# Second attention on one Trainium2 core: value products of two k-tiles side by side, row sums from the exponentials on GpSimd and VectorE

## The chip, the cores and the metric

The kernel runs on 1 core of one Trainium2 chip. The metric is the device time of one launch in microseconds (us). Both kernels get the same inputs and must return the same output.

## The reference, cut to what matters

The program is two transformer layers on a 2048 x 512 matrix. Each layer has a layer norm, an attention and a second branch. The change is in the second layer's attention (`_L1_ffn_ref`), which has 16 heads of 32 columns:

```python
scores = jnp.einsum('bhtd,bhsd->bhts', Qf, Kf) * scale
causal = jnp.tril(jnp.ones((Tx, Tx), dtype=bool))
scores = jnp.where(causal[None, None], scores, jnp.finfo(scores.dtype).min)
attn = jax.nn.softmax(scores, axis=-1)
out = jnp.einsum('bhts,bhsd->bhtd', attn, V)
y = out.transpose(0, 2, 1, 3).reshape(Bx, Tx, C)
return y @ Wp
```

T is 2048 and the batch is 1. All of it is float32.

## The kernel before, in words

The stages follow each other, each in a block of its own: `project0` and `ternary_mlp`, the first attention (`attention` with ATTN0, tiles named a_, about 566 to 1530 us), `project_out`, `gated_cumsum` and `project1` (to about 2004 us), the second attention (`attention` with ATTN1, about 2020 to 2717 us, also named a_), and `project_out` once more (w_). Both attentions use one function.

The second attention has 8 groups of 2 heads. Each group runs two passes over the scores.

Pass 1 finds the row maxima. A block is (g, i, kc): the 128 queries of tile i against up to 512 keys of chunk kc, both heads. TensorE writes the scores of both heads into one of two 128 x 1024 PSUM tiles ps_1 (`max_scores`, L620, with the causal mask added by L628 on the diagonal), and VectorE reduces them to 128 x 2 maxima (`maxima`, L706). There are 320 blocks. After each chunk c of 4 query tiles, `flip` (L637) turns the maxima into rows, `take_rows` (L723, L725) splits them, and SyncE carries them through DRAM into two extra rows of q (`put_rows`, L515, L520). So pass 2 gets scores with the maximum already taken off.

Pass 2 has 320 steps (g, c, t): 512 queries of chunk c against the 128 keys of tile t, t from 0 to 4c+3, so 4, 8, 12 and 16 steps for the four chunks and 40 for a group. In the last four steps of a chunk (the diagonal) only 512, 384, 256 and 128 columns remain (`first_col`). In a step TensorE writes transposed scores for each head into one of three PSUM tiles (`scores`, L649, mask L654), ScalarE takes the exponential into one of 6 SBUF tiles ex (L601), and TensorE multiplies with v (`times_v`, L668), one step behind. v_st has 64 columns for a head (VW=64): 32 of v and 32 ones. So each product writes 64 rows of ps_o: 32 of output and 32 copies of the row sum. The two heads of a step use rows 0 to 63 and 64 to 127. At a chunk's end ScalarE copies ps_o to SBUF (`stage`, L589); SyncE stores output and one sum row a head (L529, L530), loads the sums again as 128 x 8 (L539), VectorE inverts them (L733), SyncE stores them (L545); `project_out` reads them.

The order on each engine is written out. TensorE runs in step s: scores of head 0, the pass 1 block n = s + LEAD, scores of head 1, value products of step s-1. LEAD is 21: 21 blocks run ahead of step 0 and none are left for the last 21 steps. VectorE runs the maxima in the same order. `max_scores` waits until the block two places before has been reduced (`taken1`). All DMAs of the stage are on SyncE's queue. GpSimd does nothing in it after three memsets (L578).

In the first attention (HG=4, VW=32) a step has four heads, and each product writes 32 rows of ps_o: four column groups of TensorE in one `times_v`.

Of the kernel before, what the change touches and what calls it, by code (L numbers as in the profile page):

```python
# [14 lines left out]
F32 = mybir.dt.float32  # L15
# [22 lines left out]
ATTN0 = dict(HG=4, KH=1, VH=1, DH=16, VW=32, SCALE=16 ** -0.5, GROUPS=8, HALVES=2)  # L38
ATTN1 = dict(HG=2, KH=2, VH=2, DH=32, VW=64, SCALE=32 ** -0.5, GROUPS=8, HALVES=1)
QK0 = 768  # L40
# [78 lines left out]
def project0(nc, keep, A, X, xh, xl, ones_mean, eps, D):  # L119


    with ExitStack() as ctx:
# [46 lines left out]
        summed = sem("summed")  # L169
        sums_done = sem("sums_done")  # L170

# [155 lines left out]
        def _(dve):  # L327
# [56 lines left out]
            dve.wait_ge(summed, n_pieces)  # L384
            dve.tensor_reduce(A["abs_sums"][:, :], parts[:, :, :], AX.X, ALU.add).then_inc(sums_done, 1)

# [17 lines left out]
def attention(nc, shared, name, cfg, D, n_layer, neg_ident, mask):  # L404
# [42 lines left out]
    with ExitStack() as ctx:  # L447
# [247 lines left out]
        def _(dve):  # L695
# [39 lines left out]
            for s in range(-1, len(STEP_LIST) + Z_DELAY + 1):  # L735
                for n in SLOTS.get(s, ()):
                    if n in FLIP_AT:
                        take_rows(n)
                    if n < len(BLOCKS):
                        maxima(n)  # L740
                        g, i, kc, p = BLOCKS[n]
                        if LAST_BLOCK[g, i // TPC] == n:
                            whole_max(g, i // TPC, n)
                if s - Z_DELAY in LAST_STEP:
                    invert(*LAST_STEP[s - Z_DELAY])
# [443 lines left out]
def project1(nc, keep, reused, xh, xl, D):  # L1189


    with ExitStack() as ctx:
# [20 lines left out]
        ol = [sb(f"ol{i}", [P, CH], F32R) for i in range(NO)]  # L1213
        v_sb = [sb(f"v{i}", [P, H, 2 * DH]) for i in range(2)]
        bank = [psum(f"bank{i}", [P, CH]) for i in range(NB)]
# [11 lines left out]
        out_done = [sem(f"out_done{i}") for i in range(NO)]  # L1227
        v_ones = sem("v_ones")
        v_mapped, v_staged = sem("v_mapped"), sem("v_staged")
# [28 lines left out]

        @block.gpsimd
        def _(pool):  # L1260
            for b in range(2):
                last = pool.memset(v_sb[b][:, :, DH:2 * DH], 1.0)
            last.then_inc(v_ones, 1)

        @block.scalar
        def _(act):
            act.wait_ge(w_in[2], 16)
            act.activation(wh[2][:, :, :], w[2][:, :, :], ACT.Copy).then_inc(w_high, 1)
            act.wait_ge(prep, 1)
            act.activation(roots[:, :, :], clipped[:, :, :], ACT.Sqrt).then_inc(rooted, 1)  # L1270
            act.wait_ge(v_ones, 1)
            for t in range(QT):
                if t == QT // 2:
                    act.wait_ge(tails, 6)
                    for i in range(2):
                        act.activation(wh[i][:, :, :], w[i][:, :, :], ACT.Copy).then_inc(w_high, 1)
                act.wait_ge(v_mapped, t + 1)
                if t >= 2:
                    act.wait_ge(v_out[t % 2], 32 * (t // 2))
                act.activation(v_sb[t % 2][:, :, 0:DH], v_bank[t % 2][:, :].rearrange("p (h d) -> p h d", h=H), ACT.Copy)\  # L1280
                    .then_inc(v_staged, 1)
            for n in range(len(tiles)):
                act.wait_ge(mapped, n + 1)
                if n >= NO:
                    act.wait_ge(out_done[n % NO], 32 * (n // NO))
                act.activation(oh[n % NO][:, :], bank[n % NB][:, :], ACT.Copy).then_inc(high_done, 1)
# [60 lines left out]
def build(nc, D):  # L1347
# [15 lines left out]
    with ExitStack() as keep, ExitStack() as ctx:  # L1363
# [76 lines left out]
        with ExitStack() as inner:  # L1440
# [3 lines left out]
            project1(nc, keep, reused, xh, xl, D)  # L1444
        attention(nc, shared, "a1", ATTN1, D, 1, neg_ident, masks[1])
        project_out(nc, shared, "w1", 16, X, D["o1"], D["z1"], D["wp"], D["out"])
# [52 lines left out]
```

## Time and profile before

| | us |
|---|---|
| median of 3 runs | 2812.28 |
| lowest, highest | 2808.53, 2830.82 |
| the profiled execution's own time | 2813.36 |
| its span, first to last instruction | 2811.6 |
| TensorE busy | 2538.1 (90%) |
| VectorE busy | 1513.4 (54%) |
| ScalarE busy | 1233.2 (44%) |
| GpSimd busy | 100.2 (4%) |

PE is TensorE's matmul, PEld its weight load, DVE VectorE, ACT ScalarE, POOL GpSimd, SP SyncE. A float32 matmul stands as two records (two weight loads, two matmuls); the ones of type float32r as one. Matmul ends are modelled, so what a matmul costs its engine is read from start to start.

### The profile page before, as it was taken

Reading aid. Unit: us, or ns where it says so; the run is one execution under the profiler, and the core shown is the slowest. Engines: PE = TensorE matmul, PEld = TensorE weight load, DVE = VectorE, ACT = ScalarE, POOL = GpSimd, SP = SyncE. Lnnn points to the kernel's source line nnn. Section 1 sums busy time; section 2 is a strip of 40 time slices with the busy share of each in tenths; the row PEclk is TensorE's granted clock in tenths of the full one; section 3 lists DMA queues with packets and bytes.
Section 4 is the critical chain, followed back from the end, with each engine's and each line's share of the span. In section 5 each row is a group of like instructions: output and inputs, shape, how many; then the busy total and the mean of one; then the engine's idle time right before and its main releaser. Section 6 shows DMA issues by size and latency. Waiting matters only on the chain. (4 is left out here: it accounts for less than half of the span.)

```text
span 2811.6 us, 36071 instructions
## 1 busy us (share of the span) xinstructions
PE 2538.1 (90%) x14242; PEld 1586.1 (56%) x14242; DVE 1513.4 (54%) x1702; ACT 1233.2 (44%) x2325; POOL 100.2 (4%) x89
## 2 busy tenths in 40 slices
PE   4959999769999999999997689979699999999966
PEld 2748888645555555555552557768554544454525
DVE  3644544466877778678760444331255555555513
ACT  2422222205776767667763132122145555555541
POOL 1210000100000000000000012210100000000000
PEclk8979999956999989899985889989789999999988
DMA  3761100052122122020000410047732212220024
GB/s 132 232 203 45 45 30 15 12 69 28 30 33 36 24 39 37 15 48 8 6 10 13 127 59 1 1 109 199 202 81 68 55 37 51 69 70 8 10 58 141
DMA packets 121872, 172.68 MB, mean 61 GB/s; under 512 B 61360, under 2 KB 67120, under 8 KB 115312
## 3 DMA queue, kind: packets, MB, share of 16 engines
q1 hardware_dynamic: 118256, 157.91, 22.9%
q10 hardware_dynamic: 3456, 12.58, 1.4%
q8 instruction: 106, 1.74, 0.3%
q14 instruction: 54, 0.44, 0.1%
HBM read 118.38 MB, written 51.90 MB: 61 GB/s over the span
## 5 line engine op out<-in xcount | busy, mean ns | idle before, releaser
L601 ACT ACTIVATE a_ex<-a_ps_s 128x512 f32<-128x512 f32 (+3 forms) x1920 | 943.1, 536 | 721.8 <-PE a_ps_s L654 391.2
L706 DVE TENSOR_REDUCE a_mx_part<-a_ps 128x2 f32<-128x1024 f32 (+1 forms) x960 | 993.8, 1062 | 490.4 <-PE a_ps L620 258.6
L649 PE MATMUL a_ps_s<-a_q,a_k 50*128 50x512 f32 (+7 forms) x1920 | 766.1, 449 | 4.6 <-ACT a_ex L601 3.8
L620 PE MATMUL a_ps<-a_k,a_q 48*128 48x512 f32 (+6 forms) x1920 | 627.0, 443 | 75.1 <-DMA a_q<-q 51.8
L649 PEld LDWEIGHTS a_ps_s<-a_q,a_k 50*128 50x128 f32 (+1 forms) x1920 | 355.5, 199 | 535.0 <-ACT a_ex L601 425.7
L668 PE MATMUL a_ps_o<-a_ex,a_v 128*32 128x512 f32 (+7 forms) x3840 | 641.7, 586 | 0.5 <-ACT a_o L589 0.5
L620 PEld LDWEIGHTS a_ps<-a_k,a_q 48*128 48x128 f32 (+1 forms) x1920 | 318.0, 203 | 139.3 <-DVE a_mx_part L706 57.8
L668 PEld LDWEIGHTS a_ps_o<-a_ex,a_v 128*32 128x32 f32 (+1 forms) x3840 | 116.0, 120 | 140.7 <-ACT a_ex L601 98.1
L654 PEld LDWEIGHTS a_ps_s<-mask_half_k,mask_sel_k 64*128 64x128 f32 x1024 | 168.8, 200 | 4.2
L654 PE MATMUL a_ps_s<-mask_half_k,mask_sel_k 64*128 64x64 f32 x1024 | 158.3, 247 | 0.0
L628 PEld LDWEIGHTS a_ps<-mask_half_q,mask_sel_q 64*128 64x128 f32 x1024 | 149.6, 212 | 1.6
L628 PE MATMUL a_ps<-mask_half_q,mask_sel_q 64*128 64x64 f32 x1024 | 142.3, 256 | 0.0
L110 PE MATMUL w_ps<-w_oh,w_wh 128*128 128x512 f32 x128 | 53.2, 416 | 72.8 <-DVE w_ol L996 72.8
L110 PE MATMUL gc_bank<-xh,gc_wh 128*128 128x512 f32 x256 | 103.7, 405 | 16.3 <-DVE xl L100 16.3
L919 DVE TENSOR_TENSOR mlp_hid<-mlp_ps_g,mlp_act_up 128x512 f32<-128x512 f32 x64 | 44.2, 690 | 132.9 <-PE mlp_ps_g L833 123.5
L832 PE MATMUL mlp_ps_u<-xh,mlp_w 128*128 128x512 f32 x256 | 101.1, 395 | 16.0 <-DVE mlp_w L897 16.0
L870 ACT ACTIVATE mlp_act_up<-mlp_ps_u,mlp_s 128x512 f32<-128x512 f32 x64 | 44.2, 690 | 158.7 <-PE mlp_ps_u L833 158.7
L844 PE MATMUL mlp_ps_y<-mlp_hh,mlp_w 128*128 128x512 f32 x256 | 102.1, 399 | 1.5 <-DVE mlp_hl L922 1.5
L111 PE MATMUL gc_bank<-xl,gc_wh 128*128 128x512 f32 x256 | 101.8, 397 | 0.0
L112 PE MATMUL gc_bank<-xh,gc_wl 128*128 128x512 f32 x256 | 101.6, 397 | 0.0
L833 PE MATMUL mlp_ps_u<-xl,mlp_w 128*128 128x512 f32 x256 | 100.9, 394 | 0.0
L845 PE MATMUL mlp_ps_y<-mlp_hl,mlp_w 128*128 128x512 f32 x256 | 100.1, 391 | 0.0
(161 smaller groups left out, 2605.1 us busy)
## 6 DMA issues: line engine op xcount, KB each, us to landing
a_q<-q SPq DMA_DIRECT2D x48, 256.0 KB, 5.3
a_k<-k SPq DMA_DIRECT2D x24, 512.0 KB, 5.9
a_q<-q SPq DMA_DIRECT2D x24, 512.0 KB, 7.5
q<-p_oh SPq DMA_DIRECT2D x32, 256.0 KB, 2.5
q<-p_ol SPq DMA_DIRECT2D x32, 256.0 KB, 2.8
w_o<-o SPq DMA_DIRECT2D x8, 1024.0 KB
w_z<-z SPq DMA_DIRECT2D x32, 256.0 KB
v<-p_v SPq DMA_DIRECT2D x32, 256.0 KB, 3.4
```

Of the source, the lines that this page charges most:

```text
L110: pe.matmul(out, wh(k), xh(k), start=k == 0, stop=False)
L111: pe.matmul(out, wh(k), xl(k), start=False, stop=False)
L112: mm = pe.matmul(out, wl(k), xh(k), start=False, stop=k == KT - 1)
L601: act.activation(ex[unit % NE][:, h % 2, off:CH], ps_s[n % 3][:, off:CH], ACT.Exp, scale=SCALE)\
L620: mm = pe.matmul(ps_1[m % 2][:, e, 0:w], q_st[s][r0:r0 + KC, slot_h, i * P:(i + 1) * P], k_st[s][r0:r0 + KC, h % KH, kc * CH:kc * CH + w], ...
L628: mm = pe.matmul(ps_1[m % 2][:, e, cols], sel[r0:r0 + ROWS, part, :], low[r0:r0 + ROWS, :], start=False, stop=part == HALVES - 1)
L649: mm = pe.matmul(ps_s[n % 3][:, off:CH], k_st[st][r0:r0 + KM, h % KH, t * P:(t + 1) * P], q_st[st][r0:r0 + KM, slot_h, c * CH + off:(c + 1 ...
L654: mm = pe.matmul(ps_s[n % 3][:, cols], sel[r0:r0 + ROWS, part, :], low[r0:r0 + ROWS, :], start=False, stop=part == HALVES - 1)
L668: mm = pe.matmul(ps_o[h * CT:h * CT + VW, off:CH], v_st[g % NS][:, h % VH, t, :], ex[(s * PAIRS + h // 2) % NE][:, h % 2, off:CH], start=t ...
L706: dve.tensor_reduce(mx_part[:, 2 * p:2 * p + 2, i, kc], bank[:, :, 0:w], AX.X, ALU.max).then_inc(taken1, 1)
L832: pe.matmul(bank[n % 2][:, :], w[b][i][:, k, cols], xh[:, k, chunk(c)], start=k == 0, stop=False)
L844: pe.matmul(ps_y[:, m, :], w[b][2][:, e, cols], hh[n % 2][:, :], start=e == 0, stop=False)
```

## The change

The second attention gets a function of its own, `attention_two`. Passes, blocks, steps, score matmuls, masks and exponentials stay as they are. What differs:

- v has no ones columns (VW=32); `project1` writes and stores half as much for it.
- `times_v(d)` takes the two steps 2d and 2d+1 together: heads 0 and 1 of the even k-tile go to rows 0 to 63 of ps_o, those of the odd one to rows 64 to 127. Each chunk then has two part sums: ScalarE copies the odd half out (`odd_part`), VectorE adds it to the even half (`join`).
- Row sums: GpSimd adds head 0's exponentials into acc[.][0]; VectorE adds those of head 1 into acc[.][1], but in chunks above 0 with t % 4 == 3 GpSimd adds head 1 too, into acc[.][2]. Six slots after a chunk's last step, `sums` multiplies them with ones on TensorE into a ps_1 tile, VectorE copies it (`take_sums`), SyncE stores one row a head.
- ex has 8 tiles, LEAD1 is 24, the delays of the sums' way to and from DRAM are longer; k, q and maxima are loaded as before.

```diff
-ATTN1 = dict(HG=2, KH=2, VH=2, DH=32, VW=64, SCALE=32 ** -0.5, GROUPS=8, HALVES=1)
+ATTN1 = dict(HG=2, KH=2, VH=2, DH=32, VW=32, SCALE=32 ** -0.5, GROUPS=8)
...
+def attention_two(nc, shared, name, cfg, D, n_layer, neg_ident, mask):
...
+    LEAD1 = 24
...
+    NE = 8
+    NZ = 4
+    Z_AFTER, Z_LOAD, Z_DELAY = 6, 12, 22
...
+    def pool_adds(s):
+
+        g, c, t = STEP_LIST[s]
+        return c > 0 and t % TPC == TPC - 1
...
+        @block.gpsimd
+        def _(pool):
...
+            for s, (g, c, t) in enumerate(STEP_LIST):
+                j, off, tile = g * NCH + c, first_col(c, t), ex[s % NE]
+                pool.wait_ge(exp_done, (s + 1) * HG)
+                if t == 0 and j >= 2:
+                    pool.wait_ge(scores1, SUMS_ENTRY[j - 2] + 1)
+                for h, total in ((0, acc[j % 2][0]), (1, acc[j % 2][2]))[0:1 + pool_adds(s)]:
+                    if done > 0:
+                        pool.wait_ge(added0, done)
...
+                    if t == 0 or (h, t) == (1, TPC - 1):
+                        pool.tensor_copy(total[:, :], tile[:, h, :]).then_inc(added0, 1)
+                    else:
+                        pool.tensor_tensor(total[:, off:CH], total[:, off:CH], tile[:, h, off:CH], ALU.add).then_inc(added0, 1)
+                    done += 1
...
+            def odd_part(g, c, d):
...
+                act.activation(o_odd[j % 2][:, c0:CH], ps_o[OR:P, c0:CH], ACT.Copy).then_inc(odd_out, 1)
...
+                    if h == 0 and s >= NE:
+                        act.wait_ge(pv_done, (s - NE) // 2 + 1)
+                        act.wait_ge(added0, adds_through(s - NE, True))
+                        act.wait_ge(added1, adds_through(s - NE, False))
...
+            def sums(n):
+
+                j, m = SUMS_AT[n], sums_entry(n)
+                s, c = n - LEAD1 - Z_AFTER, j % NCH
+                pe.wait_ge(taken1, m - 1)
+                pe.wait_ge(added0, adds_through(s, True))
+                pe.wait_ge(added1, adds_through(s, False))
+                bank = ps_1[m % 2]
+                pe.matmul(bank[0:DH, 0, :], one[:, :], acc[j % 2][0][:, :], start=True, stop=True)
+                mm = pe.matmul(bank[DH:OR, 0, :], one[:, :], acc[j % 2][1][:, :], start=True, stop=c == 0)
+                if c > 0:
+                    mm = pe.matmul(bank[DH:OR, 0, :], one[:, :], acc[j % 2][2][:, :], start=False, stop=True)
+                mm.then_inc(scores1, 1)
...
+            def times_v(d):
...
+                for odd in range(2):
+                    t, s = t0 + odd, 2 * d + odd
+                    off = first_col(c, t)
+                    for h in range(HG):
+                        r0 = odd * OR + h * DH
+                        mm = pe.matmul(ps_o[r0:r0 + DH, off:CH], v_st[g % NS][:, h, t, :], ex[s % NE][:, h, off:CH],
+                                       start=t0 == 0, stop=last)
+                mm.then_inc(pv_done, 1)
...
+                scores(s, 0)
+                entries(s + LEAD1)
+                scores(s, 1)
+                if s % 2 == 1 and s > 1:
+                    times_v(s // 2 - 1)
...
+            def take_sums(n):
...
+                dve.tensor_copy(z_sb[j % 2][:, :], ps_1[m % 2][0:OR, 0, :]).then_inc(taken1, 1)
+
+            def add_ex(s):
+
+                g, c, t = STEP_LIST[s]
+                j, off = g * NCH + c, first_col(c, t)
+                total, tile = acc[j % 2][1], ex[s % NE][:, 1, off:CH]
+                if pool_adds(s):
+                    return
+                dve.wait_ge(exp_done, (s + 1) * HG)
...
+                if t == 0:
+                    dve.tensor_copy(total[:, :], tile).then_inc(added1, 1)
+                    return
+                dve.wait_ge(added1, adds_through(s - 1, False))
+                dve.tensor_tensor(total[:, off:CH], total[:, off:CH], tile, ALU.add).then_inc(added1, 1)
+
+            def join(g, c):
...
+                dve.tensor_tensor(o_sb[j % 2][:, c0:CH], ps_o[0:OR, c0:CH], o_odd[j % 2][:, c0:CH], ALU.add)\
+                    .then_inc(staged, 1)
...
+            for s in range(-1, len(STEP_LIST) + Z_DELAY + 1):
+                if s - 4 in LAST_STEP:
+                    join(*LAST_STEP[s - 4])
+                for n in slots(s):
...
+                    if n < len(BLOCKS):
+                        maxima(n)
...
+                if 0 <= s - 2 < len(STEP_LIST):
+                    add_ex(s - 2)
...
-        attention(nc, shared, "a1", ATTN1, D, 1, neg_ident, masks[1])
+        attention_two(nc, shared, "a1", ATTN1, D, 1, neg_ident, masks[1])
```

## Rows read from the trace of the kernel before

In the views by stretch (groups 1 and 8) a row is: from:to and length in us; busy us (instructions) of PE, PEld, DVE, ACT and POOL; the granted TensorE clock as a share of 2.4 GHz; DMA share; GB/s. In order of time a row is: start, us, engine, line, operation, output<-input, shapes, count, and in brackets the idle time before it and what ended it. In the views by line: busy us, mean ns, idle us.

**Rows 1.** Busy time by stretch, second attention: loop with maxima, tail without.

```profile
2049.00:2672.00 623.00, 623.00 (x2890) 315.95 (x2890) 341.04 (x411) 325.08 (x620) 0.00 (x0) 0.99 0.21 48
2672.00:2717.00 45.00, 42.81 (x182) 16.38 (x180) 6.18 (x11) 26.21 (x52) 0.00 (x0) 1.00 0.03 5
```

**Rows 2.** Order of time, TensorE, second attention.

```profile
2317.53 1.08 PE L668 MATMUL a_ps_o<-a_ex,a_v 128*64 128x512 f32 x4
2318.54 0.50 PE L649 MATMUL a_ps_s<-a_q,a_k 98*128 98x512 f32 x1
...
2326.26 0.87 PE L668 MATMUL a_ps_o<-a_ex,a_v 128*64 128x384 f32 x4
2327.06 0.33 PE L649 MATMUL a_ps_s<-a_q,a_k 98*128 98x128 f32 x1
```

**Rows 3.** Order of time, TensorE, first attention: four heads in four column groups.

```profile
1002.82 1.06 PE L668 MATMUL a_ps_o<-a_ex,a_v 128*32 128x512 f32 x8
1003.81 0.50 PE L649 MATMUL a_ps_s<-a_q,a_k 50*128 50x512 f32 x1
```

**Rows 4.** Order of time, TensorE: four float32 products of 512 columns, eight records, in series.

```profile
1745.24 3.59 PE L57 MATMUL gc_mean<-X,ones_mean 128*128 128x512 f32 x8
```

**Rows 5.** VectorE by form and in order of time: the maxima of the lead, single operations.

```profile
2036.13 2.41 DVE L706 TENSOR_REDUCE a_mx_part<-a_ps 128x2 f32<-128x1024 f32 x2 [0.45 <-PE a_ps L620]
2038.58 0.19 DVE L712 TENSOR_REDUCE a_mx<-a_mx_part 128x8 f32<-128x32 f32 x1
2038.68 2.40 DVE L706 TENSOR_REDUCE a_mx_part<-a_ps 128x2 f32<-128x1024 f32 x2
...
103.55 1.29 DVE L355 TENSOR_TENSOR p_rot<-p_prod 128x512 f32<-128x512 f32 x2
...
L706 DVE TENSOR_REDUCE a_mx_part<-a_ps 128x2 f32<-128x256 f32 x30 | 12.8, 426 | 14.7 <-PE a_ps L628 14.7
L994 DVE TENSOR_TENSOR w_o<-w_o,w_z 128x2048 f32<-128x2048 f32 x8 | 18.3, 2291 | 37.3 <-DMA w_z<-z 37.3
L1302 DVE COPY p_col<-p_roots 128x384 f32<-128x384 f32 x1 | 0.4, 362 | 0.0
```

**Rows 6.** GpSimd in order of time and by line: adds of 128 x 512, others.

```profile
1681.98 1.29 POOL L1183 TENSOR_TENSOR gc_z<-gc_state,gc_qg 128x512 f32<-128x512 f32 x1 [11.73 <-DVE gc_qg L1171]
1683.35 1.30 POOL L1186 TENSOR_TENSOR X<-X,gc_z 128x512 f32<-128x512 f32 x1
...
L1262 POOL MEMSET p_v<- 128x512 f32 x2 | 1.0, 533 | 0.3 <-POOLq L1018 0.3
L1426 POOL TENSOR_SCALAR_AFFINE_SELECT neg_ident<-neg_ident 128x128 f32<-128x128 f32 x1 | 0.3, 294 | 0.2 <-POOL raw_mask L1413 0.2
```

**Rows 7.** Order of time, GpSimd and VectorE at work together, in three places.

```profile
1694.17 2.28 DVE L100 TENSOR_TENSOR xl<-gc_xc,xh 128x2048 fp32r<-128x2048 f32 x1
1694.39 3.22 POOL L1183 TENSOR_TENSOR gc_z<-gc_state,gc_qg 128x512 f32<-128x512 f32 x1 [9.74 <-DVE gc_qg L1171]
1696.56 2.29 DVE L64 TENSOR_TENSOR gc_xc<-X,gc_mean 128x2048 f32<-128x2048 f32 x1
1697.69 1.29 POOL L1186 TENSOR_TENSOR X<-X,gc_z 128x512 f32<-128x512 f32 x1
...
160.95 2.50 POOL L235 TENSOR_TENSOR p_ol<-p_rot,p_oh 128x512 fp32r<-128x512 f32 x2 [8.19 <-ACT p_oh L292]
162.33 1.67 DVE L355 TENSOR_TENSOR p_rot<-p_prod 128x512 f32<-128x512 f32 x1 [3.85 <-POOL p_ol L235]
```

**Rows 8.** Busy time by stretch, first attention: end of its maxima, tail, one dip.

```profile
1458.00:1466.00 8.00, 7.41 (x58) 4.07 (x59) 0.97 (x5) 5.59 (x12) 0.00 (x0) 1.00 0.02 3
1466.00:1518.00 52.00, 48.72 (x180) 14.38 (x181) 0.25 (x1) 27.73 (x57) 0.00 (x0) 0.53 0.02 4
1144.00:1160.00 16.00, 16.00 (x80) 7.95 (x79) 8.73 (x11) 8.35 (x16) 0.00 (x0) 0.50 0.11 29
```

More of the change, by code:

```diff
@@ L169, in project0 @@
         summed = sem("summed")
-        sums_done = sem("sums_done")
         tiles = [(c, j) for c in range(NCH) for j in range(5)]
@@ L384, in _ @@
             dve.wait_ge(summed, n_pieces)
-            dve.tensor_reduce(A["abs_sums"][:, :], parts[:, :, :], AX.X, ALU.add).then_inc(sums_done, 1)
+            dve.tensor_reduce(A["abs_sums"][:, :], parts[:, :, :], AX.X, ALU.add)
 PASS2_STEPS = [(c, t) for c in range(NCH) for t in range(TPC * (c + 1))]
@@ L1213, in project1 @@
         ol = [sb(f"ol{i}", [P, CH], F32R) for i in range(NO)]
-        v_sb = [sb(f"v{i}", [P, H, 2 * DH]) for i in range(2)]
+        v_sb = [sb(f"v{i}", [P, H, DH]) for i in range(2)]
         bank = [psum(f"bank{i}", [P, CH]) for i in range(NB)]
@@ L1227, in project1 @@
         out_done = [sem(f"out_done{i}") for i in range(NO)]
-        v_ones = sem("v_ones")
         v_mapped, v_staged = sem("v_mapped"), sem("v_staged")
@@ L1257, in _ @@
                 sp.wait_ge(v_out[b], 32 * QT // 2)
[L1259 to L1263, printed above, removed]
         @block.scalar
@@ L1270, in _ @@
             act.activation(roots[:, :, :], clipped[:, :, :], ACT.Sqrt).then_inc(rooted, 1)
-            act.wait_ge(v_ones, 1)
             for t in range(QT):
@@ L1279, in _ @@
                     act.wait_ge(v_out[t % 2], 32 * (t // 2))
-                act.activation(v_sb[t % 2][:, :, 0:DH], v_bank[t % 2][:, :].rearrange("p (h d) -> p h d", h=H), ACT.Copy)\
+                act.activation(v_sb[t % 2][:, :, :], v_bank[t % 2][:, :].rearrange("p (h d) -> p h d", h=H), ACT.Copy)\
                     .then_inc(v_staged, 1)
```

276 lines of the change are left out of this document (added).

## The prediction

> **What bounds the kernel now.** I read the page first, for the stages, and then the busy time by stretch. In the second attention's loop TensorE is busy for all of 623 us, VectorE for 341, ScalarE for 325, GpSimd for none [rows 1]. The reader is to see that TensorE alone sets this stage, at its full clock. The stretch from 2049 to 2672 us holds 296 steps, each with a block of maxima; the last 24 of the 320 run to 2716. Then I read TensorE's order of time for what one piece costs, start to start, since ends are modelled. The two heads' value products of a full step take 2318.54 - 2317.53 = 1.01 us, with 384 columns 0.80 [rows 2]; 256 and 128 columns go on in the same steps of 0.21: 0.58 and 0.37. Last I read VectorE and GpSimd where they work at once elsewhere in the program [rows 7], because the change loads both.
>
> **The change on TensorE.** A group of heads has 40 steps: 28 of 512 columns and 4 each of 384, 256 and 128. Value products now: 28 x 1.01 + 4 x (0.80 + 0.58 + 0.37) = 35.3 us a group. After it four products of 32 rows stand in four column groups, as in the first attention, where that takes 1003.81 - 1002.82 = 0.99 us [rows 3]. So a pair of steps costs what one step did: 12 full pairs and 4 of 512 with 384 columns at 0.99, and 4 of 256 with 128 at 0.58: 18.2 us, 17.1 less. The sums add float32 products of the accumulators. A lone one costs 3.59 / 4 = 0.9, from which a modelled end goes off: 0.86 [rows 4]. Two in different column groups are 1.0; the third of chunks 1 to 3 goes into the second's group and follows it: 1.86. That is 1.0 + 3 x 1.86 = 6.6 us a group. TensorE's group of 623 / 7.4 = 84.2 us becomes 84.2 - 17.1 + 6.6 = 73.7. If nothing else were late, 296 steps (7.4 groups) would gain 10.5 x 7.4 = 78 us.
>
> The Trainium skill ("TensorE: Matmul & The Clock Gate", Part 3 on packing small matmuls) gives a speed-up of 2.38 for three products of 32 output rows and 512 columns side by side. As an estimate by it three would cost 0.86 x 3 / 2.38 = 1.08 us, and four no less, which adds 1.4 us or more a group to TensorE; the row with four in 0.99 us decides.
>
> **The change on VectorE.** Back to back, a full reduction costs 1.20 us and the 256-wide form 0.40 (its 0.43 less the overlap); 512 and 768 lie between, 0.67 and 0.93 [rows 5]. A group has 28 full ones and 4 of each narrower: 41.6 us. An add of two SBUF tiles of 512 columns is 0.69 us alone and 0.60 behind another (two take 1.29); with 2.29 for 2048 columns, 384, 256 and 128 columns are 0.47, 0.34 and 0.20 [rows 5]. VectorE gets head 1 except where GpSimd takes it: per group 18 full adds, 4 of 384, 4 of 256, 1 of 128 and 4 copies (bounds 0.36, a copy of 384 columns, and 0.69, an add; I take 0.35 since the nearest row is a copy): 10.8 + 3.4 + 1.4 = 15.6 us. The rest of a group: four each of taking the rows (2 x 0.3), copying the sums (0.6) and joining (0.6), a fifth short piece, and 0.19 each for whole maximum and reciprocal: 9.0. Together 66.2 us, below TensorE's 73.7. If VectorE only had these times, it would stay hidden.
>
> **GpSimd, and what the two do to each other.** Dependent GpSimd adds of 512 columns start 1683.35 - 1681.98 = 1.37 us apart [rows 6]. Narrower ones aren't in the trace: between 0.29 (a 128 x 128 select) and 1.29; on a line between these 1.0, 0.7 and 0.4. A copy lies between a memset's 0.53 and an add's 1.29; I take 0.7, nearer the memset, for it has one operand to read. Per group GpSimd has 27 full adds, 4 x 2.1 and 3 x 0.4 of narrow ones, 7 copies: 37.0 + 8.4 + 1.2 + 4.9 = 51.5 us.
>
> Two engines don't add at the same time. A GpSimd add begun 0.22 us into a VectorE operation with two SBUF inputs took 3.22 us instead of 1.29, that is, until that was over and then its own time; beside one with a PSUM input it took 1.29 [rows 7]. The other way round: VectorE's add at 162.33 took 1.67, so it began at 163.31, when GpSimd's ended at 163.45 [rows 7]. GpSimd thus shuts VectorE's adds out for about 1.29 - 0.14 = 1.15 us of each 1.37. The maxima read PSUM and are not concerned. GpSimd's 51.5 us are at most 43 of shutting out; over 77 us that is 0.56 of the time, and a VectorE add that meets it waits half of 1.15: 0.32 us on average. Bounds: 0 (always in a gap) and 1.15. I take 0.32, as neither engine is timed to the other. 31 adds and copies: 9.9 us. VectorE's group is 76.1 us: more than TensorE's 73.7. Two orders are tied to it: behind a waiting add stand the next maxima, and TensorE's block two places on waits for them (two ps_1 tiles).
>
> The Trainium skill ("SBUF — State Buffer", on the two sides of SBUF) calls the shared port pair an exclusive lock, taken also by a VectorE copy in a two-port mode. No row shows such a copy beside GpSimd; by the page the 4 copies a group wait too, which is how they are counted here; were they free, the sum would fall by 4 x 0.32 x 7.4 = 9 us.
>
> GpSimd itself needs 51.5 + 14.3 (VectorE's adds at 0.55 of holding and the narrow ones) = 66 us a group, so it isn't late on average; eight ex tiles let it lag in the long chunks, where it has 29 us for 16 steps.
>
> **The sum.** Loop: 7.4 x 76.1 = 563 us. In front of each sums entry VectorE runs dry: TensorE has 1.86 + 0.66 + 0.99 us of other work against two filled tiles (2.4). I take 0.6 us, 28 times: 17 (bounds 0 and 1.1 us). 580 against 623: -43. Tail, 24 steps without maxima: GpSimd's work (14 + 29 us with VectorE's adds between) is as long as the 44 us now; the clock may fall there as in the first attention's tail [rows 8]: +2 (0 to 10). Lead: 24 blocks instead of 21, at 1.27 us each (2038.68 - 2036.13 is two and a whole maximum) [rows 5]: +4. End: behind the last exponential now come a product and a copy (L668, L589); afterwards GpSimd's last two adds, 1.86 of products and a copy before the same DMAs: +3 (0 to 8). ScalarE: 64 rows instead of 128 in its copy change nothing, and it is hidden (325 of 580). Half as much v to write, store and load lies beside TensorE's products: 0, and no more than 1 us if that cover went. SyncE: two stores a chunk fewer, hidden. Sum -34: 2813.4 - 34 = **2779 us**. The profiled execution is 1.1 us above the median shown, so either basis gives the same.
>
> **Rivals.** (1) TensorE stays the bound: adds fall into gaps. For it: VectorE without waits has 66 us a group against 74. Against it: waits above 0.24 us end it. Time: -78 + 4 + 3 + 2 gives 2744. Chance 0.23. (2) VectorE waits long and drags TensorE along: slower. Where GpSimd lags behind, its next add follows in 0.1 us, and VectorE's add finds it always at work; then the mean wait goes to 0.7 us or more. Price: (0.7 - 0.32) x 31 x 7.4 = 87 us, 2866. It decides from a mean wait of 0.47 us on, where the gain of 34 us is gone. For it: 29 us of GpSimd's work in 16 steps of chunk 3. Against it: chunks 0 and 1 leave it idle. Chance 0.20. (3) The clock. TensorE with pauses may be granted 1.2 GHz for stretches. Rows: 0.50 in a stretch of the first attention's loop in which it was busy throughout, and 0.53 in its tail, right after steps in which it had first had short pauses [rows 8]; against it: the second attention never fell so far [rows 1]. At 1.2 GHz a group is near 130 us; a tenth of the loop so costs 0.74 x (130 - 78) = 38 us: 2817. Chance 0.15. (4) The products of the odd tile don't run beside the even ones: then pairs cost two, 17 us a group come back and TensorE is at 91: +50 us; the first attention's rows speak against it, and I count it in (2).
>
> **How the numbers follow.** My own case has 0.42, and spreads from 2755 to 2808 (waits 0.25 to 0.42, VectorE's dry times 0 to 1.1 us). The range from 2738 to 2848 leaves out most of (2) and the edge of (1). 1% is 28 us, about what a measurement of this kernel can tell from no change. Faster by more: 0.23 of (1), 0.26 of my case, 0.03 of (3): 0.52. Slower by more: 0.15 of (2), 0.04 of (3): 0.19. Within: 0.29.
>
> **What would show it.** Right: value products of a pair spaced 0.99 us; in the loop TensorE idle for some 5%, released by the maxima; VectorE's adds with means near 1.0 us where 0.69 is their own, GpSimd's adds above 1.29; the loop near 580 us. Wrong: TensorE at 100% and the loop near 545 (1), or VectorE's adds at 1.3 us and more and the loop above 630 (2), or a granted clock below 0.95 in the loop (3).

## The result and the profile after

The changed kernel takes 2857.51 us (median of 4, 2851.66 to 2877.62) against 2820.36 us before: ratio 1.0146, 95% interval 1.0076 to 1.0216. It is slower by 1.5%; 2779 us were forecast, and the range ended at 2848.

The profiled execution of the changed kernel has a span of 2849.9 us, 38.3 more than before. The lead, from the stage's first product to its first exponential, is 31.9 us against 28.0 (forecast 4 more). From the start of the first to the start of the last exponential of the second attention it is 689.5 us (2743.8 - 2054.3) against 664.7 (2714.9 - 2050.2), 25 more, where 626 were forecast (580 and 46). From the last exponential's start to the end of the span it is 106.1 us (2849.9 - 2743.8) against 96.7 (2811.6 - 2714.9), 9 more. So most of the loss is in the loop. Busy time by stretch over that whole attention in whole microseconds, the changed kernel (columns as in [rows 1]):

```profile
2054.00:2745.00 691.00, 628.29 (x3230) 330.41 (x3228) 561.62 (x735) 337.36 (x671) 421.37 (x386) 0.90 0.17 40
```

TensorE is busy for 38 us less than before (665.81 us of the 667 from 2049 to 2716), though part of it ran at half clock, and idle for 63. The granted clock has a mean of 0.90, where [rows 1] have 0.99 and 1.00. The reader is to ask where it idles; the view of waits of 2060 to 2700 us tells (waiting line <- releaser: us in total, times, longest):

```profile
POOL a_acc L946 <- PE a_ps L1019: 47.1, 7, 7.6
PE a_ps_o L1050 <- DVE a_o L1145: 46.2, 29, 2.1
...
PEld a_ps L994 <- DVE a_mx_part L1091: 30.9, 50, 1.7
...
PE a_ps L994 <- DVE a_mx_part L1091: 11.1, 14, 1.4
```

The second row is the one that the prediction doesn't have: at each chunk's start the first value products wait for VectorE's `join` of the chunk before, since ps_o is free only then. Over all 31 chunk starts it is 49.2 us, 1.6 each. (The first row, GpSimd's waits for the sums, turns out in the run e8_acc3 to cost nothing.) TensorE, in order of time, at one of them:

```profile
2141.19 0.38 PE L1005 MATMUL a_ps<-neg_ident,a_mx 128*8 128x128 f32 x2
2143.00 0.73 PE L994 MATMUL a_ps<-a_k,a_q 96*128 96x512 f32 x2 [1.42 <-DVE a_mx_part L1091]
...
2146.16 1.91 PE L1050 MATMUL a_ps_o<-a_ex,a_v 128*32 128x512 f32 x8 [1.35 <-DVE a_o L1145]
2148.00 0.80 PE L1030 MATMUL a_ps_s<-a_q,a_k 98*128 98x512 f32 x1
```

VectorE meanwhile: the join stands behind a block of maxima and a copy of exponentials, though ScalarE's half was ready at 2144.95:

```profile
2143.76 1.23 DVE L1091 TENSOR_REDUCE a_mx_part<-a_ps 128x2 f32<-128x1024 f32 x1 [0.32 <-PE a_ps L994]
2144.91 0.52 DVE L1131 COPY a_acc<-a_ex 128x512 f32<-128x512 f32 x1
2145.34 0.67 DVE L1145 TENSOR_TENSOR a_o<-a_ps_o,a_o_odd 64x512 f32<-64x512 f32 x1
```

On average over the 31 starts the odd half was ready 0.06 us before TensorE came to its wait, the join began 0.80 us after that, took 0.64 itself, and TensorE went on 0.15 later. So half of the pause is VectorE's other work, and half is the join itself.

And the clock, by stretches of 1 us:

```profile
2145.00:2146.00 1.00, 0.00 (x0) 0.00 (x0) 1.00 (x3) 0.42 (x2) 0.59 (x2) 1.00 0.00 0
2146.00:2147.00 1.00, 0.84 (x7) 0.23 (x8) 0.81 (x3) 0.00 (x0) 0.00 (x0) 0.60 0.68 131
2147.00:2148.00 1.00, 1.00 (x8) 0.00 (x0) 0.00 (x0) 0.00 (x0) 0.00 (x0) 0.50 0.44 139
2148.00:2149.00 1.00, 1.00 (x4) 0.83 (x3) 0.00 (x0) 0.16 (x1) 0.00 (x0) 0.50 1.09 276
2149.00:2150.00 1.00, 1.00 (x4) 0.60 (x2) 0.31 (x1) 0.47 (x2) 0.00 (x0) 0.69 1.00 297
2150.00:2151.00 1.00, 1.00 (x6) 0.27 (x6) 1.00 (x2) 1.00 (x2) 0.00 (x0) 1.00 1.15 254
```

Right after the pause it falls to 0.50, that is 1.2 GHz, for 3.4 us, and the eight products that take 0.99 us take 1.84 (2148.00 - 2146.16). In such 1-us stretches the attention has 160 us below 0.95, in 23 pieces. The first, 14 us, is the end of a stretch at 1.2 GHz that began before the stage, and every run has such a piece (6 to 28 us). The other 22, 146 us, stand each behind a pause of TensorE of 1.3 us or more and last 3.4 to 10.2 us; the kernel before has none of them. (The expectations below say 228 and 4 us: those are counted in stretches of 4 us, and a stretch counts whole when only a part of it was low.)

The 9 us at the end are mostly a wait too. TensorE's last sums products wait for GpSimd's last add:

```profile
2751.25 1.03 PE L1016 MATMUL a_ps<-a_acc,a_one 128*32 128x512 f32 x1 [6.12 <-POOL a_acc L948]
```

What was forecast of the pieces, in rows of the changed kernel. A pair of steps at full clock, in order of time, answers [rows 3] with 0.99 us, and three sums products, two side by side and the third behind them, answer [rows 4] with 2118.91 - 2117.07 = 1.84 us:

```profile
2185.34 1.06 PE L1050 MATMUL a_ps_o<-a_ex,a_v 128*32 128x512 f32 x8
2186.33 0.50 PE L1030 MATMUL a_ps_s<-a_q,a_k 98*128 98x512 f32 x1
...
2117.07 0.62 PE L1016 MATMUL a_ps<-a_acc,a_one 128*32 128x512 f32 x1
...
2117.96 1.02 PE L1019 MATMUL a_ps<-a_acc,a_one 128*32 128x512 f32 x2
2118.91 0.73 PE L994 MATMUL a_ps<-a_k,a_q 96*128 96x512 f32 x2
```

The adds by form (busy us, mean ns, idle before) answer [rows 5, 6]:

```profile
L948 POOL TENSOR_TENSOR a_acc<-a_acc,a_ex 128x512 f32<-128x512 f32 x216 | 301.2, 1394 | 158.0 <-ACT a_ex L973 143.9 <-POOL a_acc L948 0.4
L1134 DVE TENSOR_TENSOR a_acc<-a_acc,a_ex 128x512 f32<-128x512 f32 x144 | 138.9, 964 | 1.6 <-ACT a_ex L973 0.8
L946 POOL COPY a_acc<-a_ex 128x512 f32<-128x512 f32 x56 | 36.9, 659 | 106.9 <-ACT a_ex L973 50.8 <-PE a_ps L1019 47.1 <-PE a_ps L994 6.2
...
L1131 DVE COPY a_acc<-a_ex 128x512 f32<-128x512 f32 x32 | 26.1, 817 | 0.0
```

### The profile page after: what moved, and what is told of

It reads as the page before. It is cut to its first block and busy times, and to the rows that moved or that the text cites. A ratio compares the mean times of both kernels' runs of the same rounds, so it can differ in the third digit from the quotient of the medians.

```text
span 2849.9 us, 38069 instructions
## 1 busy us (share of the span) xinstructions
PE 2509.2 (88%) x14418; PEld 1586.2 (56%) x14418; DVE 1733.5 (61%) x2023; ACT 1219.1 (43%) x2325; POOL 525.8 (18%) x479
## 5 line engine op out<-in xcount | busy, mean ns | idle before, releaser
L705 DVE TENSOR_REDUCE a_mx_part<-a_ps 128x2 f32<-128x1024 f32 (+3 forms) x640 | 652.9, 1060 | 205.4 <-PE a_ps L627 101.6
L648 PE MATMUL a_ps_s<-a_q,a_k 50*128 50x512 f32 (+3 forms) x1280 | 493.7, 458 | 4.0 <-ACT a_ex L600 3.8
L619 PE MATMUL a_ps<-a_k,a_q 48*128 48x512 f32 (+3 forms) x1280 | 425.2, 465 | 49.9 <-DMA a_q<-q 29.1
L948 POOL TENSOR_TENSOR a_acc<-a_acc,a_ex 128x512 f32<-128x512 f32 (+1 forms) x336 | 389.9, 1160 | 203.3 <-ACT a_ex L973 179.6
L648 PEld LDWEIGHTS a_ps_s<-a_q,a_k 50*128 50x128 f32 x1280 | 234.2, 203 | 307.6 <-ACT a_ex L600 227.0
L1091 DVE TENSOR_REDUCE a_mx_part<-a_ps 128x2 f32<-128x1024 f32 (+2 forms) x320 | 335.3, 1054 | 84.5 <-PE a_ps L994 52.0
L667 PE MATMUL a_ps_o<-a_ex,a_v 128*32 128x512 f32 (+3 forms) x2560 | 338.1, 604 | 0.0
L994 PE MATMUL a_ps<-a_k,a_q 96*128 96x512 f32 (+3 forms) x640 | 234.1, 435 | 38.3 <-DMA a_q<-q 23.4
L619 PEld LDWEIGHTS a_ps<-a_k,a_q 48*128 48x128 f32 x1280 | 203.2, 204 | 92.8 <-DVE a_mx_part L705 48.0
L1030 PE MATMUL a_ps_s<-a_q,a_k 98*128 98x512 f32 (+3 forms) x640 | 253.2, 434 | 1.2 <-ACT a_ex L973 1.1
L1050 PE MATMUL a_ps_o<-a_ex,a_v 128*32 128x512 f32 (+3 forms) x1280 | 169.4, 581 | 49.2 <-DVE a_o L1145 49.2
```

The costliest lines, as they stand in the source:

```text
L619: mm = pe.matmul(ps_1[m % 2][:, e, 0:w], q_st[s][r0:r0 + KC, slot_h, i * P:(i + 1) * P], k_st[s][r0:r0 + KC, h % KH, kc * CH:kc * CH + w], ...
L648: mm = pe.matmul(ps_s[n % 3][:, off:CH], k_st[st][r0:r0 + KM, h % KH, t * P:(t + 1) * P], q_st[st][r0:r0 + KM, slot_h, c * CH + off:(c + 1 ...
L667: mm = pe.matmul(ps_o[h * CT:h * CT + VW, off:CH], v_st[g % NS][:, h % VH, t, :], ex[(s * PAIRS + h // 2) % NE][:, h % 2, off:CH], start=t ...
L705: dve.tensor_reduce(mx_part[:, 2 * p:2 * p + 2, i, kc], bank[:, :, 0:w], AX.X, ALU.max).then_inc(taken1, 1)
L948: pool.tensor_tensor(total[:, off:CH], total[:, off:CH], tile[:, h, off:CH], ALU.add).then_inc(added0, 1)
L994: mm = pe.matmul(ps_1[m % 2][:, h, 0:w], q_st[s][0:KC, h, i * P:(i + 1) * P], k_st[s][0:KC, h, kc * CH:kc * CH + w], start=True, stop=not ...
```

## The experiments

Two theories stood after the result. C: the loss is TensorE's pause at chunk starts and the clock after it. L: it is VectorE's load, its adds stretched by GpSimd's (rival 2). "Loop" below is from the start of the first to the start of the last exponential, "low" the us of it in 1-us stretches with a granted clock below 0.95, and "first" the part of low in the piece at the loop's start, which no change of the loop made. Loop and low come from one traced execution of each run.

Medians of different sessions are not quite comparable. The kernel before, run beside each, had 2807.7 to 2820.4 us (e15, e16, e17 and e6_again ran on another chip than the rest), and in the traces the stage begins anywhere from 2012 to 2044 us, after work that all the kernels share. So the ratio says more than the median, and the loop more than either.

| run | median us | ratio to before, 95% | loop | low | first |
|---|---|---|---|---|---|
| before |  |  | 665 | 6 | 6 |
| the change | 2857.5 | 1.0146 (1.0076 to 1.0216) | 690 | 160 | 14 |
| e1_join | 2785.2 | 0.9906 (0.9862 to 0.9950) | 630 | 80 | 26 |
| e2_nopool | 2763.6 | 0.9849 (0.9780 to 0.9918) | 618 | 67 | 28 |
| e3_nodve | 2759.7 | 0.9835 (0.9769 to 0.9900) | 593 | 16 | 12 |
| e4_noadds | 2745.4 | 0.9784 (0.9725 to 0.9842) | 600 | 35 | 27 |
| e6_early | 2772.9 | 0.9822 (0.9729 to 0.9915) | 610 | 56 | 20 |
| e6_again | 2774.3 | 0.9859 (0.9772 to 0.9946) | 601 | 28 | 12 |
| e7_join_early | 2772.9 | 0.9804 (0.9719 to 0.9890) | 608 | 44 | 20 |
| e8_acc3 | 2772.4 | 0.9811 (0.9707 to 0.9914) | 603 | 28 | 12 |
| e9_fill | 2811.8 | 0.9958 (0.9919 to 0.9996) | 642 | 43 | 13 |
| e10_early_noadds | 2709.8 | 0.9657 (0.9594 to 0.9720) | 561 | 14 | 14 |
| e11_early_nopool | 2724.9 | 0.9697 (0.9678 to 0.9716) | 563 | 12 | 12 |
| e16_early_flipfill | 2752.8 | 0.9790 (0.9713 to 0.9868) | 600 | 26 | 22 |
| e13_before_pause | 2869.3 | 1.0210 (1.0144 to 1.0277) | 713 | 28 | 7 |
| e14_before_pause_fill | 2853.0 | 1.0149 (1.0129 to 1.0168) | 703 | 7 | 7 |
| e15_before_pause2 | 2998.6 | 1.0670 (1.0594 to 1.0747) | 828 | 283 | 7 |
| e17_before_pause2_fill | 2877.3 | 1.0236 (1.0162 to 1.0310) | 722 | 6 | 6 |

**e1_join: TensorE waits for ScalarE instead of VectorE.**

```diff
                 act.activation(o_odd[j % 2][:, c0:CH], ps_o[OR:P, c0:CH], ACT.Copy).then_inc(odd_out, 1)
+                act.activation(o_sb[j % 2][:, :], ps_o[0:OR, :], ACT.Copy).then_inc(odd_out, 1)
...
-                    pe.wait_ge(staged, g * NCH + c)
+                    pe.wait_ge(odd_out, 2 * (g * NCH + c))
```

> ScalarE copies both halves of ps_o out (one copy more a chunk, 32 in all) and TensorE's next chunk waits for ScalarE, not for VectorE's join; VectorE joins two SBUF tiles. Theory C (TensorE pauses at the chunk ends behind VectorE's backlog, and its clock falls after them): the 49 us of waits for the join go and some dips of the clock with them; the kernel gets 30 to 60 us shorter, near 2805, granted clock in the loop above 0.92. Theory L (VectorE's load with its waits for GpSimd sets the loop): VectorE has the same work, so within 10 us of the changed kernel, near 2855.

2785 us: 72 us less than the change (67 by the ratios), with one more copy a chunk; theory C had said 30 to 60. The waits at chunk starts were 21.5 us (29 times, 0.7 each), and the low stretches behind the first fell from 146 to 54 us. Theory L had given no such gain.

**e2_nopool, e3_nodve, e4_noadds: the adds left out** (GpSimd's, VectorE's, both; the row sums are then not, or only partly, computed), the late join kept. The waits for the adds that are gone go too.

```diff
-                pool.tensor_copy / pool.tensor_tensor of every step
...
-                    add_ex(s - 2)
```

> GpSimd's adds and copies are left out (its accumulators are filled once; the row sums of head 0 and part of head 1 are missing from the result). VectorE's adds stay and have the port alone. Theory L: VectorE's adds fall from a mean of 0.96 us to 0.69 and the loop by 50 us or more, kernel near 2795. Theory C: the adds fall too, but VectorE still has its backlog at chunk ends, so the dips stay: 15 to 30 us less, near 2830.

> VectorE's adds and copies of exponentials are left out (the row sums of head 1 are mostly missing from the result), GpSimd's stay. VectorE then has about 50 us a group against TensorE's 74: both theories say TensorE sets the loop at 74 x 8 = 590 us plus the end, kernel near 2750. If it stays above 2790, GpSimd or the sums entries cost time by themselves (its wait for the accumulator of two chunks before was up to 7.6 us).

> No adds on either engine (all row sums are missing); products side by side, the sums' matmuls, join and rows stay. Both theories: TensorE bound, loop near 590 us, kernel near 2745. The difference to the run without VectorE's adds alone is what GpSimd costs by itself: 0 by both theories, up to 20 us if its late accumulators hold anybody.

All three are 94 to 112 us below the change (84 to 102 by the ratios). e3 and e4 came out as forecast; e2, at 2764, came out below what either theory had said (2795 and 2830). The wait for the join is 33.5, 31.9 and 31.1 us in them, 1.0 to 1.1 each instead of 1.6: this much is in the order of the work itself (the join stands a step too late; in all three it takes 0.65 us of the wait itself, and the odd half is ready 0.14 us after TensorE comes), and the rest is VectorE's backlog. Either engine's adds left out takes the backlog away, so these runs alone don't part the price of the adds from that of the pauses.

**e6_early, e7_join_early, e8_acc3, e6_again: copy and join one step earlier.** e6 is the changed kernel with these two lines and their calls moved:

```diff
-                if s - 4 in LAST_STEP:
-                    odd_part(*LAST_STEP[s - 4], (s - 4) // 2)
+                if s - 3 in LAST_STEP:
+                    odd_part(*LAST_STEP[s - 3], (s - 3) // 2)
...
-                if s - 4 in LAST_STEP:
-                    join(*LAST_STEP[s - 4])
+                if s - 3 in LAST_STEP:
+                    join(*LAST_STEP[s - 3])
```

> The changed kernel with ScalarE's copy of the odd half and VectorE's join one step earlier in their orders (before the exponentials and maxima of the third step of the next chunk instead of the fourth); nothing else moves. Theory C (the loss is TensorE's pause at the chunk's first value products behind VectorE's backlog, and the clock after it): TensorE's wait for the join falls from 49 us to under 15 us, the share of the loop below full clock from 228 us to about 100, and the time from 2857 to about 2790 to 2810. Rival L (VectorE is simply too busy, its adds stretched by GpSimd's): the backlog only moves to the maxima, TensorE waits there instead, and the time stays above 2845.

> Both halves copied out by ScalarE, as in the run e1_join (2785 us), and these copies and the join one step earlier. Theory C: the 20 us that TensorE still waits for ScalarE's copies at 28 chunk starts go, and with them part of the 108 us below full clock: 2760 to 2775 us. Rival: the pauses that remain are those behind the maxima, and the time stays at 2785 within 8 us.

> As e7_join_early, and a third set of accumulators for head 0 and head 1 (the room comes from keeping v for two groups instead of three, so v is loaded one group later), so that GpSimd and VectorE may begin a chunk before the sums of the chunk two back are taken. Theory C, with GpSimd's 7 waits of up to 7 us for those sums as a source of lag that later holds ScalarE and TensorE: 5 to 15 us faster than e7_join_early. Rival: GpSimd has slack enough (busy 64% of the loop), the waits are off the path, and the time is that of e7_join_early within 5 us.

> e6_early again on the same chip as e16, to compare the two: 2773 us within 5.

Not one operation was added or removed in e6, and it is 85 us faster than the change (theory C had said 47 to 67), and faster than the kernel before (ratio 0.982). Its busy time by stretch and its wait at chunk starts:

```profile
2049.00:2659.00 610.00, 584.41 (x3222) 315.12 (x3224) 554.35 (x735) 334.37 (x671) 421.86 (x384) 0.96 0.19 45
```

```profile
PE a_ps_o L1050 <- DVE a_o L1145: 2.8, 7, 0.4
```

VectorE's 554 and GpSimd's 422 us are those of the change (562, 421): both are as loaded as in the change, and only the pause is gone. That excludes L as the cause of the slowdown. e7 came out in theory C's range (2773), but it is no faster than e6: ScalarE's second copy is of no more use then. e8 is within 1 us of e7, so GpSimd's waits for the sums of the chunk two back (34 us in e6) are off the path, as its rival said.

**e9_fill: the pause left as it is, but filled.** Six score products whose results are overwritten, some 43 us of work in all (186 of 0.23 us, start to start):

```diff
                 if t0 == 0 and g * NCH + c > 0:
+                    pe.wait_ge(exp_done, fs * HG - 2)
+                    for _ in range(6):
+                        pe.matmul(ps_s[fs * HG % 3][:, foff:CH], ..., start=True, stop=True)
                     pe.wait_ge(staged, g * NCH + c)
```

> The changed kernel with its waits as they are; but just before TensorE waits for the join at a chunk's start it issues six more score products of 512 columns (float32r, about 0.22 us each, results overwritten by the next step's scores): about 1.3 us of work in the place of a pause of 1.6 us on average, 31 times, 41 us of added work in all. Clock theory (most of the loss is the clock granted after a pause, not the pause): TensorE's wait shrinks to under 15 us, the 228 us of the loop below full clock fall to under 120, and the time falls from 2857 to about 2800 though work was added. Rival (a pause costs its own length and the clock falls for another reason, such as the mix of products in the diagonal): the clock's share stays near 228 us and the time is 2850 to 2870.

```profile
2061.00:2703.00 642.00, 621.62 (x3410) 343.23 (x3410) 558.87 (x735) 336.71 (x671) 417.65 (x385) 0.97 0.19 43
```

The join keeps its place in VectorE's order and nothing is taken away. TensorE's wait for it falls from 49.2 to 6.7 us, by as much as was added in products; still it is 46 us faster than the change (2812, where the theory had about 2800), with 160 low us become 43. So the clock is a cost of its own, apart from the pause. What is left low here is the first piece, and one of 3.4 us behind each of 7 pauses of 1.4 us for maxima.

**e10_early_noadds, e11_early_nopool: what the adds cost without the pauses.** As e6, with all adds, or GpSimd's, left out (row sums not, or only partly, computed).

> The changed kernel with copy and join one step earlier (e6_early, 2773 us), and no row sums at all: neither GpSimd nor VectorE adds exponentials, the sums' products and their copies stay. It shows what is left of the adds' price once TensorE doesn't pause at chunk starts. Theory C (TensorE nearly sets the pace now, VectorE's adds cost it only the waits behind the maxima, 68 us of idle time in e6_early): 10 to 35 us faster than e6_early, 2740 to 2765 us. Rival L (the adds and their collisions are the main price): 50 us faster or more, below 2725.

> As e6_early, but GpSimd's adds left out and VectorE's kept, so that VectorE's 144 adds and copies run at their own length (in e2_nopool 608 and 417 ns instead of 892 and 817). The difference to e6_early is the price of the two engines excluding each other. Theory C: 5 to 20 us faster than e6_early. Rival L: 40 us and more faster.

Here theory C was too low. By medians e10 is 63 us faster than e6 and e11 48, which is what L had said. By the ratios it is 46 and 35 us against e6_early, 57 and 46 against e6_again, so L's bounds (50 and 40) are near the truth, and no more can be said. The loop is 561 and 563 us, so VectorE's own adds cost the loop nothing. GpSimd's cost it 38 to 47 us (601 and 610 in two profiles of the same kernel), though GpSimd itself is late only once in e6's loop (ScalarE waits 1.4 us for it). A part of these 38 to 47 us is again pause and clock: e6 has 7 pauses of 1.4 us behind the maxima, and 16 to 36 low us behind the first piece, where e10 and e11 have neither. VectorE's adds and copies in e11, by form:

```profile
L1120 DVE TENSOR_TENSOR a_acc<-a_acc,a_ex 128x512 f32<-128x512 f32 x144 | 98.1, 681 | 7.1 <-ACT a_ex L956 6.5
...
L1117 DVE COPY a_acc<-a_ex 128x512 f32<-128x512 f32 x32 | 13.0, 408 | 0.0
```

Beside GpSimd's adds they are 970 and 742 ns in e6; the maxima, which read PSUM, stay as they are. The Trainium skill ("SBUF — State Buffer", section "SBUF: two separate sides") calls the port pair of the two engines an exclusive lock, which a VectorE copy in a two-port mode takes too. The copies, 742 against 408 ns, agree with it: they wait as adds do. The trace doesn't show in which mode a copy ran, so that it is this lock is argued. At the end, from the last exponential's start to the end of the span, e10 and e11 have 98 us and e6 has 109, 9.0 of them TensorE's wait for GpSimd's last add. The 15 us between the medians of e10 and e11 are not in this stage: in their traces loop and end are alike, and the stage begins 18.7 us later in e11.

**e13 to e17: a pause put into the kernel before.** ScalarE's copy of ps_o at a chunk's end moves behind the step's two exponentials; in e15 it is made twice; in e14 and e17 five and seven score products stand ahead of TensorE's wait.

```diff
-                if s - 2 in LAST_STEP:
+                if s - 2 in LAST_STEP and HALVES > 1:
                     stage(*LAST_STEP[s - 2], s - 2)
...
                         .then_inc(exp_done, 1)
+                if s - 2 in LAST_STEP and HALVES == 1:
+                    stage(*LAST_STEP[s - 2], s - 2)
...
+                if HALVES == 1:
+                    act.activation(o_sb[j % 2][:, :], ps_o[:, :], ACT.Copy).then_inc(twice, 1)
+                    act.wait_ge(twice, j + 1)
```

(The last three lines are e15's and e17's.)

> The kernel before, second attention only: ScalarE's copy of ps_o at a chunk's end stands behind both exponentials of the step instead of ahead of them, so that TensorE's first value products of each chunk wait some 1.2 us, 31 times, 37 us in all; no work is added or taken. Clock theory (a pause at that place brings down the granted clock for some us after it, in any kernel): over 50 us slower than the kernel before, about 2880, and 60 us or more of the second attention's loop below full clock (4 us in the kernel before). Rival (a pause costs its own length): 25 to 40 us slower, about 2850, the loop's clock at 1.00 but for a few us.

> As e13_before_pause, and in the place of most of the wait five more score products of 512 columns, as in e9_fill (their results are overwritten): 31 times some 1.1 us of work. Clock theory: the loop stays at full clock and the time is that of the kernel before plus the waits' own length, 30 to 45 us slower than it, clearly faster than e13_before_pause. Rival: the same as e13_before_pause or slower.

> As e13_before_pause, with ScalarE's copy of ps_o made twice in the second attention, so that TensorE's pause at each chunk's start is about 1.9 us instead of 1.27. In e13 27 pauses of 1.2 to 1.3 us stood in the loop and only 1 was followed by a fall of the clock; in the changed kernel and in e9_fill nearly all of 1.4 us and more were. Theory (the pause's length decides, in any kernel): most of the 31 pauses are followed by a fall, 120 us or more of the loop run below full clock (27 us in e13), and the time is 20 us for the longer waits and some 40 to 50 us for the clock above e13: 2925 to 2945. Rival (it is something of the changed kernel's mix, not the pause): below full clock stay under 40 us and the time is 2885 to 2895.

> As e15_before_pause2, and seven more score products of 512 columns just ahead of the wait, which leave some 0.4 us of it. Theory: the loop stays at full clock but for under 20 us, and the time is 2865 to 2880, that is 50 us or more below e15 though 48 us of products were added. Rival: the time of e15 within 10 us.

The waits at the chunk starts of e13:

```profile
PE a_ps_o L670 <- ACT a_o L589: 38.8, 31, 1.5
```

and of e15:

```profile
PE a_ps_o L674 <- ACT a_o L593: 58.3, 31, 2.2
```

In e13 the loop is 49 us longer than before, 39 of them the pauses. The clock theory had the time right (58 us up, where it said over 50) and the clock wrong: 28 low us, not 60. That is the count of the traced execution, the fastest of three, with a mean granted clock of 0.913 over the whole kernel; the other two took 13 and 29 us more, at 0.908 and 0.901. e14, with the pause filled, is 41 us above the kernel before, as forecast; its loop is 10 us shorter than e13's, and its three executions lie within 2 us (2852 to 2854) where e13's spread over 29. In e15 the pauses are only 20 us longer in sum, 1.9 instead of 1.25 each, and the loop is 115 us longer than e13's, with 283 low us instead of 28. Its median, 2998.6, is over 50 us above what the theory had said. One of its pauses, TensorE in order of time:

```profile
2209.21 0.40 PE L655 MATMUL a_ps_s<-a_q,a_k 98*128 98x512 f32 x1
2211.50 1.97 PE L674 MATMUL a_ps_o<-a_ex,a_v 128*64 128x512 f32 x4 [1.90 <-ACT a_o L593]
2213.40 0.80 PE L655 MATMUL a_ps_s<-a_q,a_k 98*128 98x512 f32 x1
```

The products of 1.01 us [rows 2] take 1.90. With the wait filled (e17) 107 us of the loop come back, though some 50 us of products were added (217 of 0.23 us); the time, 2877, is within the theory's range, and its stretch has the full clock:

```profile
2057.00:2780.00 723.00, 717.24 (x3284) 371.23 (x3283) 346.25 (x421) 373.23 (x703) 0.00 (x0) 1.00 0.18 41
```

So it is no matter of the changed kernel's mix of products. The table counts the pauses that TensorE came to at full clock, and how many of them were followed by a fall (it begins in the pause or up to 2.4 us behind it):

| run | pause, us | times | followed by a fall |
|---|---|---|---|
| e13 | 1.16 to 1.27 | 30 | 3 |
| e13 | 1.52 | 1 | 1 |
| e15 | 1.8 to 2.2 | 24 | 24 |
| the change | 1.35 | 4 | 4 |
| the change | 1.4 to 1.5 | 15 | 6 |
| the change | 1.7 | 8 | 8 |
| the change | 2.1 | 8 | 4 |
| e6 | 1.4 | 7 | 5 |
| e6_again | 1.4 | 7 | 3 |
| e9 | 1.4 | 7 | 7 |

(The expectation of e15 counts 1 fall in e13; its trace has four, and at 2327.25 us the products take 1.79 us behind a pause of 1.27.)

```profile
2327.25 1.86 PE L670 MATMUL a_ps_o<-a_ex,a_v 128*64 128x512 f32 x4 [1.27 <-ACT a_o L589]
2329.04 0.80 PE L651 MATMUL a_ps_s<-a_q,a_k 98*128 98x512 f32 x1
```

Longer pauses are followed by falls more often in one and the same kernel (e13 against e15). But length alone doesn't decide: in the change all four pauses of 1.35 us, each of which follows a pause of 1.4 within 2 us, brought the clock down, and only half of those of 2.1 us did. What tells the one kind from the other stays open.

**e16_early_flipfill: e6, and the pause behind chunk 2's flip filled** with five products, eight times.

```diff
                     flip(n)
+                    if s >= 0 and FLIP_AT[n] % NCH == 2:
+                        pe.wait_ge(exp_done, n1 - 2)
+                        for _ in range(5):
+                            pe.matmul(ps_s[n1 % 3][:, :], ..., start=True, stop=True)
```

> The changed kernel with copy and join one step earlier (e6_early, 2773 us), and five more score products behind the transpose of chunk 2's maxima (once a group, 8 in all), where TensorE pauses 1.43 us for VectorE's maxima. In e6 3 of 5 pauses of 1.4 us and more were followed by a fall. Theory: the stretches below full clock after the first (36 us in e6) fall to under 20 us, and the time is 5 to 10 us below e6. Rival: no difference beyond 3 us.

2753 us against 2774 for e6_again on the same chip. The intervals (0.971 to 0.987 and 0.977 to 0.995) overlap, and the two profiles have the same loop within 1 us (600 and 601), so a gain over e6 isn't shown. The clock did as the theory said: no pause of 0.95 us or more is left, and 4 low us behind the first piece, where e6_early has 36 and e6_again 16. By the ratio e16 is the fastest version with the full output, 2.1% below the kernel before; e1, e6, e7, e8 and e9 are below it too, by 0.4 to 2.0%.

## Why the prediction was wrong

The step that failed is in the part on VectorE: "four each of taking the rows (2 x 0.3), copying the sums (0.6) and joining (0.6)". The join was priced as VectorE's work and nothing more. The prediction names what waits behind VectorE's adds (the next maxima and TensorE's block two places on), and not that `times_v` of the next chunk waits for `staged`, with the join behind a block of maxima. That is a wait on TensorE's path, 31 times 1.6 us: 49 us. The kernel before has the same wait, for ScalarE's copy, and it cost nothing there, since ScalarE has slack (busy 351 of 667 us) and its copy stood at the right step (moved by two exponentials, in e13, it does cost); the change gave the release to VectorE, busy 562 of 691 us, a step later than it had to be. By order alone it would be 1.0 us (e2 to e4), 0.65 of it the join's own length; VectorE's backlog makes it 1.6.

On it sits rival 3, the clock, which had a chance of 0.15 and 2817 us. The mechanism was right and its size was not: priced as a tenth of the loop, it was 160 of 691 us (143 us by the exact times), because nothing in the prediction supplied regular pauses. Undoing the pause gives back 85 us: 46 us are the pause (49.2 - 2.8), and the rest goes with the 104 low us more that the change has. That the clock explains this rest is an estimate: at half clock, at most half of them, 52 us, were lost. e9 shows it without the estimate: 46 us less, with the pause only replaced by work of the same length.

Point by point, of the rest:

- TensorE's pairs: 0.99 us forecast and measured. Its pace: 73.7 us a group forecast; without adds (e10) the 296 steps with maxima take 529 us, 71.5 a group. The sums were priced right: three products take 1.84 us and two 0.98, where I had 1.86 and 1.0.
- VectorE's adds of 512 columns: 0.60 + 0.32 = 0.92 us forecast, 0.964 measured; copies 0.67 against 0.82. The 0.60 is from start to start, though, and 0.964 is a mean length; alone such an add is 0.681 long (e11), so its mean wait is 0.28 us. That is right to 0.04 us, and rival 2, which needed 0.7 us, fell. A copy waits 0.41 (0.817 - 0.408).
- VectorE as the bound, with 2.4 us a group over TensorE: not shown as put. With GpSimd's adds TensorE is idle 26 of 610 us in e6, and the loop loses 38 to 47 us by them; I had 73 us of waits, of which TensorE's own pace hid a part. The loop of e6, 601 to 610 us, stands between the 626 forecast and the 591 of rival 1.
- GpSimd: adds 1.39 us against 1.29 alone, 421 us busy in all; "isn't late on average" held (e8). At the very end it is late, by 6.1 us.
- Lead +4: measured 3.9. End +3 (0 to 8): measured 9, just outside, by that wait.
- The sum, 34 us less, is near what e6 does: its ratio of 0.982 and 0.986 in two comparisons is 0.988 in the prediction (2779 / 2812). The prices of the single pieces were sound, and one edge of the order was missing. That the sums agree so well is in part luck: e6's loop is 16 to 25 us shorter than forecast, and its end 10 us longer.
- What would show it wrong was named as "the loop above 630" for rival 2 and "a clock below 0.95" for rival 3. The first alone would have misled here: the long loop comes with VectorE's adds at 0.96 us, not 1.3.

## What to carry to other kernels

When a change moves the release of a buffer from one engine to another, list who waits for that release and what stands ahead of it in the new engine's order, and price it as a wait of the bounding engine, not as work of the releasing one. If TensorE bounds the stage, pauses can cost far more than their length: here 49 us of them, 1.6 each, cost some 80 us of loop (690 - 610), and 58 us of them, 1.9 each, 163 (828 - 665), since TensorE ran at 1.2 GHz for 3.4 us and longer after many of them. Look for it in stretches of 1 us just after each wait. The cure can be an order moved by one step, worth more here (85 us) than the whole change was forecast to bring (34).

## What the runs showed of the hardware that was not expected

- The price of a pause is not proportional to it. In the same kernel 31 pauses of 1.25 us cost 49 us of loop, and 31 of 1.9 us 163 us (828.1 - 664.7).
- Useless products can pay: 50 us of them took 107 us off the loop of e15, 43 us of them 48 us off the loop of the change.
- VectorE's 8 adds of 128 columns, 0.28 us long without GpSimd's adds (e2), took 1.21 us on average in the changed kernel, and those of 512 columns 0.96 instead of 0.68: a short operation can wait longer for GpSimd than a long one.
